# A decoder layer on one core: one projection, one transpose and one output product change places where the self-attention hands over to the cross-attention, and one VectorE copy moves

## What is computed

```python
x = layernorm(x + self_attention(x))              # 16 heads of 64, no mask
x = layernorm(x + cross_attention(x, ctx, mask))  # 16 heads of 16, 375 context tokens
x = layernorm(x + ffn(x))                         # 8 routed experts (top 1) + 1 shared, SiLU gate
```

## Time and profile before

| | us |
|---|---|
| median of 3 runs (lowest, highest) | 438.15 (437.25, 438.18) |
| time of the profiled execution | 437.25 |
| span of its trace, first to last instruction | 435.5 |
| PE busy | 414.6 (95%) |
| PEld busy | 296.1 (68%) |
| DVE busy | 244.7 (56%) |
| ACT busy | 194.5 (45%) |
| POOL busy | 50.5 (12%) |

### The profile page before, as it was taken

The page is one execution under the profiler, slowest core; times in us unless marked ns, Lnnn a source line. Parts: engine busy times, 40 slices in busy tenths (PEclk is TensorE's granted clock), DMA queues, the critical chain, the costliest instruction groups (busy, mean ns, idle before and its releaser), DMA issues.

```text
span 435.5 us, 8958 instructions
## 1 busy us (share of the span) xinstructions
PE 414.6 (95%) x3125; PEld 296.1 (68%) x3126; DVE 244.7 (56%) x724; ACT 194.5 (45%) x580; POOL 50.5 (12%) x77
## 2 busy tenths in 40 slices
PE   8999999999999999999999999999989998999992
PEld 7766778778686767766766676767665474666661
DVE  1365756657566566655666676767762552244443
ACT  1164362434426446676666666767663101111110
POOL 4010010100101001000010101010100045212222
PEclk9999999999999999999999999999999999999998
DMA  8999000000000014041304221900000013122210
GB/s 253 361 382 252 12 2 2 0 2 2 1 2 0 2 38 145 2 181 25 159 24 159 68 115 47 390 38 2 2 2 2 1 50 109 48 62 69 68 38 30
DMA packets 15241, 34.22 MB, mean 79 GB/s; under 512 B 2381, under 2 KB 9150, under 8 KB 13920
## 3 DMA queue, kind: packets, MB, share of 16 engines
q1 hardware_dynamic: 13952, 30.70, 20.2%
q0 software_dynamic: 1104, 2.76, 1.8%
q10 hardware_dynamic: 144, 0.23, 0.2%
HBM read 27.24 MB, written 6.70 MB: 78 GB/s over the span
## 4 chain that ended last, share of the span: by engine, by line
PE 66%; issue 24%; DVE 6%; ACT 1%; SPq 1%; DMA 0%; POOLq 0%; POOL 0%; DVEq 0%; ACTq 0%
PE bank L434 9%; PE bank L633 7%; PE bank L504 6%; PE bank L448 6%; PE bank L615 4%; PE bank L879 4%; PE bank L855 4%; PE bank L532 3%; PE bank L491 3%; PE bank L526 3%; PE bank L861 3%; PE bank L465 3%; PE bank L649 3%; PE bank L477 2%; PE bank L518 1%
## 5 line engine op out<-in xcount | busy, mean ns | idle before, releaser
L1234 DVE CUSTOM_DVE_ANT_0 p<-bank,mask 112x375 f32<-112x375 f32 x128 | 62.7, 546 | 34.7 <-PE bank L615 34.7
L995 ACT ACTIVATE p<-p,nm 112x375 f32<-112x375 f32 x128 | 74.8, 609 | 1.6 <-DVE nm L1234 1.6
L633 PEld LDWEIGHTS bank<-ident,p 112*125 112x125 f32 x384 | 48.9, 187 | 22.9 <-issue 14.5
L1002 ACT ACTIVATE pT<-bank 125x336 f32<-125x336 f32 x96 | 42.8, 447 | 46.1 <-PE bank L633 46.1
L633 PE MATMUL bank<-ident,p 112*125 112x112 f32 x384 | 58.8, 286 | 1.0
L434 PE MATMUL bank<-x2T,arena 128*128 128x224 f32 x256 | 53.2, 355 | 0.0
L938 ACT ACTIVATE p<-bank,nm 112x112 f32<-112x112 f32 x128 | 43.5, 365 | 18.7 <-DVE nm L1105 18.6
L434 PEld LDWEIGHTS bank<-x2T,arena 128*128 128x128 f32 x256 | 46.8, 191 | 0.4 <-DMA x2T<-in_xT 0.3
L349 POOL TENSOR_TENSOR rstd<-veps,minus_half 128x1 f32<-128x1 f32 x14 | 7.7, 549 | 292.3 <-DVE veps L1131 292.3
L1098 DVE TENSOR_SCALAR arena<-bank 128x448 f32<-128x448 f32 x32 | 20.0, 624 | 25.7 <-PE bank L434 25.7
L615 PE MATMUL bank<-kT,qz 32*112 32x375 f32 x256 | 28.8, 517 | 2.6 <-ACT x2T L964 2.1
(11 more groups left out here) (140 smaller groups left out, 597.6 us busy)
## 6 DMA issues: line engine op xcount, KB each, us to landing
arena<-in_ug SPq DMA_DIRECT2D x8, 1024.0 KB, 5.2
arena<-in_dn SPq DMA_DIRECT2D x8, 512.0 KB, 6.6
mid<-in_ctxT SPq DMA_DIRECT2D x8, 375.0 KB, 3.1
slots_s<-blank SPq DMA_DIRECT2D x14, 128.5 KB, 3.9
arena<-in_wqk SPq DMA_DIRECT2D x7, 256.0 KB, 5.0
slots_x<-blank SPq DMA_DIRECT2D x14, 128.0 KB, 6.4
p<-slots_s SPq DMA_DIRECT2D x9, 128.5 KB, 2.1
kT<-slots_x SPq DMA_DIRECT2D x9, 128.0 KB
```

The source lines that it names most:

```text
L633: mm = pe.transpose(PE_T2[r][0:SK, t * S:(t + 1) * S], p2[i % RING][:, t * SK:(t + 1) * SK], ident[0:S, 0:S])
L995: act.activation(p2[i % RING], p2[i % RING], ACT.Exp, bias=nm2[:, i % H:i % H + 1], scale=-1.0).then_inc(exp2, 1)
L1002: act.activation(pT2[0:SK, i % RING], PE_T2[r][0:SK, 0:KT * S].rearrange("p (k n) -> p k n", k=KT), ACT.Copy).then_inc(pt2_act, 1)
L1234: v.tensor_tensor_reduce(p2[i % RING], PE_S2[r][0:S, 0:S2], bias[:], 1.0, 3e38, ALU.add, ALU.min, accum_out=nm2[:, i % H:i % H + 1]).then_ ...
```

## The change

Five places are edited; all else stays.

- PE, batch 7 of the first attention: the job between `turn(3, 7)` and `value1(1, 7)` is now `turn_x1(2)` (2 transposes) in place of `project_k(1, 1)` (4 matmuls). ACT's copy there changes with it, from `evac_k(1, 1)` to `evac_x1(2)`.
- PE, after the last batch: `out1(6)` now stands right behind `value1(1, 7)`, ahead of `score2(0)`; before, it stood behind `score2(0)`.
- `score2(0)` waits for three halves of k and for `x1t_sb` 3 (both job banks emptied) instead of for four halves of k.
- PE, groups 0 and 1 of the second attention: `project_k(1, 1)` takes the place behind `score2(0)` where `out1(6)` was, with a wait for `evac_o(1, 7)`, and place 2 of group 0 is empty. The wait ahead of `turn_x1(3)` becomes one for the fourth half of k. ACT copies k between the second and third exponential of group 0, and no longer copies `x1T` between the third and fourth.
- DVE, batch 7: the copy of the first transposed group, `evac_pt(0, 7)`, comes after `rowmax(3, 7)`, as in all other batches; before, it came ahead of it in this batch alone.

```diff
--- before.py
+++ after.py
@@ -562,7 +562,7 @@
                     project_k(0, 1, J)
                 else:
                     pe.wait_ge(q_sb, 1)
-                    project_k(1, 1, J)
+                    turn_x1(2, J)
 
             pe.wait_ge(consts, 3)
             for _ in range(WARM):
@@ -594,6 +594,7 @@
                 if b == 1:
                     pe.wait_ge(prep, 5)
                     pe.matmul(PE_W1[:, 0:S], anyw, ident[0:S, 0:S], start=True, stop=True).then_inc(q_any, 1)
+            out1(NT - 1)
 
 
             def score2(n):
@@ -603,7 +604,8 @@
                 if n == 0:
                     pe.wait_ge(exp1[2], B)
                     pe.wait_ge(exp1[3], B)
-                    pe.wait_ge(k_sb, 2 * KC)
+                    pe.wait_ge(k_sb, KC + 1)
+                    pe.wait_ge(x1t_sb, 3)
                 else:
                     pe.wait_ge(max2, n * STRIPS)
                 if g == 0:
@@ -677,11 +679,10 @@
             def between_first(g, place):
 
                 if (g, place) == (0, 0):
-                    out1(NT - 1)
-                if (g, place) == (0, 2):
-                    turn_x1(2)
+                    pe.wait_ge(ot1[1], B)
+                    project_k(1, 1)
                 if (g, place) == (1, 0):
-                    pe.wait_ge(x1t_sb, 3)
+                    pe.wait_ge(k_sb, 2 * KC)
                     turn_x1(3)
                 if (g, place) == (1, 2):
                     pe.wait_ge(x1t_sb, 4)
@@ -986,7 +987,7 @@
                 evac_o(0, b)
                 if b == B - 1:
                     evac_k(0, 1, PE_J1[0])
-                    evac_k(1, 1, PE_J1[1])
+                    evac_x1(2, PE_J1[1])
                 evac_o(1, b)
 
             def exps2(n, r):
@@ -1013,8 +1014,8 @@
             def between(n, place):
 
                 b, g = n // GROUPS, n % GROUPS
-                if (g, place) == (0, 1) and b == 0:
-                    evac_x1(2)
+                if (g, place) == (0, 0) and b == 0:
+                    evac_k(1, 1)
                 if (g, place) == (1, 0) and b == 0:
                     evac_x1(3)
                 if (g, place) == (1, 0) and 1 <= b < B - 1:
@@ -1190,11 +1191,8 @@
                     ln1_a(b - 2)
                 rowmax(2, b)
                 normalise(1, b)
-                if b == B - 1:
-                    evac_pt(0, b)
                 rowmax(3, b)
-                if b < B - 1:
-                    evac_pt(0, b)
+                evac_pt(0, b)
                 if b >= 2:
                     ln1_b(b - 2)
                 if b < B - 2:
```

## The result

The changed kernel takes 440.59 us (median of 6 runs, 440.20 to 441.60) against 438.14 us for the kernel before on the same chip: ratio 1.0061, 95% interval 1.0048 to 1.0076. It is 2.1 to 3.3 us slower, 2.7 by the ratio and 2.45 by the medians. In a second series it took 440.18 us against 437.99, ratio 1.0056 (1.0040 to 1.0072). The profiled execution took 441.44 us.

What follows compares the result with a forecast made beforehand. PE, busy 95% of the span, was taken to set the time. Swap and jobs 0.0, reversed overlaps +2.8 and group 1 0.0 gave 440.66 from the mean and 440.95 from the median; forecast 440.8 us, range 438.8 to 441.8.

Steps and rivals of the forecast that it cites:

- The two reversed overlaps: At the border, `out1(6)` waits for ACT's copy and `score2(0)` for DVE's masks with PE idle: +2.8 us.
- second sum, over idle times: PE's new idle time from `turn(1, 7)` to `score2(1)`: 0.33, 0.29, 0.4, 0.76 and 0.99 us, 2.8 together.
- The swap on DVE: Batch 7: the late copy delays `turn(1, 7)` by 0.53 us; with the smaller job, 0.0 up to `value1(1, 7)`, bounds -0.5 and +0.5.
- `project_k` too short for the masks: Behind `score2(0)`: 0.83 + 1.28 us of PE work beside masks of 3.10 us leaves PE idle 0.99 us.
- Group 1: Second attention: DVE still decides, so its masks and `score2(2)` move by 2.8 us with no further cost, 0.0.
- the release at 170.85: In group 1, PE's release was taken to be DVE's and to move by 2.8 us.
- No absorption: Behind the border, PE's 3.6 us of idle time does not work off the 2.8 us; absorption had chance 0.06.
- the last 0.04: Chance left for more than 442 us, such as a fall of PE's clock in the new gaps.
- two sums with +2.8: Whole time: +2.8 us on the mean of three runs gives 440.66, on the median 440.95.

Runs made afterwards that it cites:

- e3: The changed kernel with `out1(6)` back behind `score2(0)` and `project_k(1, 1)` moved to place 2 of group 0; ratio 1.0015 to the kernel before.
- e4: The kernel before with one edit, `out1(6)` ahead of `score2(0)`; ratio 1.0061 to the kernel before.
- e8: The kernel of e4 with a product of k computed and thrown away at place 0 of group 0; ratio 1.0056 to the kernel before.
- e1: The kernel before with one edit, DVE's `evac_pt(0, 7)` behind `rowmax(3, 7)`; ratio 1.0008 to the kernel before.
- e2: The changed kernel with DVE's `evac_pt(0, 7)` put back ahead of `rowmax(3, 7)`; ratio 1.0045 to the kernel before.
- e6: The changed kernel with the product of k at place 0 of group 0 computed twice; ratio 1.0061 to the kernel before.
- e7: The kernel before with DVE's `ln1_b(6)` moved behind all four masks of group 1 and the copy; ratio 0.9998 to the kernel before.
- e9: The kernel of e7 with ACT's `evac_x1(3)` and third probability copy ahead of group 1's second exponential; 437.41 us against 437.99, ratio 0.9986.

## Why the prediction was right

**The two reversed overlaps, forecast +2.8.** Right in mechanism, and nearly so in size. ACT's copy now holds `out1(6)`: its start is 163.07 on the time scale of before (164.28 - 1.21), forecast 163.28. `score2(0)` follows at 166.72, forecast 166.84; `score2(1)` at 169.97, forecast 169.95. The idle times are 0.64 and 0.89 where I had 0.76 and 0.99. e3 takes this step out and 2.05 us go; e4, and e8 with work added, make it without the other edits and get the full loss. The sizes 2.05 and 2.79 differ because the steps don't add: with the jobs exchanged, group 0 is longer even with `out1(6)` in its old place. The prediction's second sum, over idle times, came to 2.8 partly by a term that isn't there: it has 0.29 us ahead of `turn(3, 7)`, and PE shows no bracket at all there, so the idle times give 2.38.

**The swap on DVE, forecast as using up what the smaller job gives.** Right: `turn(1, 7)` loads its weights at 155.28 (156.49 - 1.21, forecast 155.27), the evacuation of q starts at 157.45 (forecast 157.5), the last copy ends 0.10 earlier than forecast and `value1(1, 7)` starts at 161.44 (forecast 161.53). e1 and e2 price it at 0.39 either way.

**`project_k` too short for the masks.** Right, by e6: 1.37 us more of PE work there delays `score2(1)` by 0.29 only.

**Group 1, forecast 0.0 beside the shift.** The result stands, but the release at 170.85 was misread. I took it for the last mask of group 1; it is ACT's `evac_x1(3)` that ends the wait for `turn_x1(4)`. That DVE decides when `score2(2)` starts is right, by its copy behind the masks, only 0.17 us later than ACT's third copy. In the change both chains move together. Behind the landmark `score2(1)` comes 2.82 us later than before (17.50 against 14.68) and `score2(2)` 2.70, so group 1 gives back 0.12, and `value1(1, 7)` comes 0.09 earlier. The two overlaps then cost 2.91, not 2.8. Each of the three is off by about 0.1, and it is luck that two of them cancel.

**No absorption.** Right. Far behind, at the first SiLU of the shared expert, the distance from the landmark is 338.69 - 153.68 = 185.01 after and 334.73 - 152.47 = 182.26 before: +2.75, as at `score2(2)`. By the measure of the Trainium skill that the prediction weighed ("Perfetto Trace Analysis", section "Identifying the Most-Contended Engine"), PE had room (296.5 us of weight loading in 439.7 us), and none of it took up the delay.

**The clock.** The prediction left a fall of the clock in the last 0.04. In both profiles of the changed kernel it is 1.00 from 150 to 200 us, so in these two executions its idle times of 0.5 to 1.1 us did not bring it about. In e4's profile, where `project_k` does not stand in the gap, it fell, and in e6's it fell behind gaps of 0.87 and 0.38 us. What sets it off in one execution and not in another stays open.

**The time.** 440.59 against 440.8, which the prediction set between two sums with +2.8, 440.66 and 440.95. The change cost 2.45 us by the medians and 2.70 inside the trace.

## What to carry to other kernels

On an engine with an order written by hand, look at each job twice: for what it waits and for whose wait it fills. Exchanging two jobs adds no work and can still cost time, because each had covered a wait that the other doesn't cover; here that was 2 to 3 us. Where a job waits for several engines, look in the kernel's text for all that it waits for, and in the timeline for when each fell due, before you shorten the one that the profile names: here the named engine and the true one lay a tenth of a microsecond apart. And compare between landmarks on both sides of an edit, since the start alone moved by up to 1.9 us between profiles.

## What the runs showed of the hardware

**The clock.** In e4's profile it fell to its half level after PE had idled for 1.79 us, and in e6's behind gaps of 0.87 and 0.38 us. The fall in e4 lasted from 171.0 to 174.2 us, and D was 0.95 more than in e8, the nearest kernel without one. The fall in e6 lasted from 177.2 to 180.6 us: the distance from the landmark was 0.68 more than after the change at `score2(2)`, ahead of the fall, and 2.25 more at the first SiLU (341.15 - 153.89 = 187.26 against 185.01), so that 1.6 us more were lost in between.

**VectorE beside GpSimd.** The same normalisation on DVE, `ln1_b(6)`, took 0.40 us with POOL at rest (e7, e9), 0.53 beside POOL's two additions (before, after) and 0.98 in e6. The first addition takes 0.74 us, the two together 1.49 (1.43 in e6). Before, the first ran from 169.04 to 169.78, and `ln1_b(6)` (from 169.40) ended at 169.93; after, it ended at 173.84, and the first addition at 173.69. In e6 the two ran from 173.14 to 174.57, and `ln1_b(6)` (from 173.74) ended at 174.72, behind both. It ends 0.15 us behind an addition each time, as if it waited for one to end. In e3 it started 0.22 us ahead of the end of the second addition (170.93, and 171.15) and took 0.41, as at rest, so that not each overlap lengthens it. The Trainium skill, "SBUF — State Buffer", section "SBUF: two separate sides", says that VectorE, when it runs in a mode that takes two ports or reads two SBUF inputs, and GpSimd share a pair of ports, and that the one that starts first has it for the whole of its instruction while the other is blocked. The ends just behind an addition agree with it, but no run here took the additions away alone, so it is read from the profile and not shown by an experiment.
